# Second layer: products of turned rows with seven weights as three fp32r products of exact halves

## The reference

```python
x = x + attn0(layernorm(x))      # 16 heads of 8, causal softmax
x = x + moe(layernorm(x))        # 8 experts, top 2, capacity, gelu
# attn1: y = LN(h)*g+b; q,k,v = y@W + b; g = sigmoid(y@Wg + bg)  (128 -> 1024 each)
#        state = decay*state + k*v;  out = g*q*state/8;  o = out@Wo + bo
#        x2 = h + o;  return x2 + gelu(LN(x2)@W1 + b1)@W2 + b2   (128 -> 512 -> 128)
x = x + attn1(layernorm(x))
# ffn1:  h = silu(x@w1.T*s1) * (x@w2.T*s2); h = gelu(h@h1.T*..); h = gelu(h@h2.T*..); h@w3.T*s3
x = x + ffn1(layernorm(x))
```

## Time and profile before

| | |
|---|---|
| median of 3 runs | 770.17 us (768.14 to 771.0) |
| the profiled execution | 770.86 us, its span 768.8 us |
| mean granted TensorE clock | 0.933 of full speed |
| busy: TensorE / VectorE / ScalarE / GpSimd | 633.4 / 398.5 / 260.2 / 141.6 us |
| the chain that ended last | TensorE 61%, VectorE 19%, issue 8%, GpSimd 6%, ScalarE 5% |

### The profile page before, as it was taken

The page is one execution under the profiler, slowest core; times in us unless marked ns, Lnnn a source line. Parts: engine busy times, 40 slices in busy tenths (PEclk is TensorE's granted clock), DMA queues, the critical chain, the costliest instruction groups (busy, mean ns, idle before and its releaser), DMA issues.

```text
span 768.8 us, 8745 instructions
## 1 busy us (share of the span) xinstructions
PE 633.4 (82%) x2992; PEld 376.8 (49%) x2992; DVE 398.5 (52%) x1008; ACT 260.2 (34%) x342; POOL 141.6 (18%) x169
## 2 busy tenths in 40 slices
PE   2579999799798408989609779999999999999997
PEld 0545556456455306777504255364545455464544
DVE  6677778777786321111046955944385616831100
ACT  2325454445345102333103214422534135412311
POOL 3002212332432540000054073011000300010000
PEclk9989999899999657999958988999999999999999
DMA  5223242342410201443110011000000000000000
GB/s 153 90 72 133 103 152 75 93 162 63 134 60 1 82 31 48 124 123 106 35 27 28 0 28 28 0 1 1 14 0 0 0 14 1 0 1 1 14 0 14
DMA packets 40900, 38.69 MB, mean 50 GB/s; under 512 B 3104, under 2 KB 31776, under 8 KB 40864
## 3 DMA queue, kind: packets, MB, share of 16 engines
q1 hardware_dynamic: 38816, 34.04, 14.3%
q0 software_dynamic: 2048, 4.20, 1.8%
HBM read 23.54 MB, written 14.68 MB: 50 GB/s over the span
## 4 chain that ended last, share of the span: by engine, by line
PE 61%; DVE 19%; issue 8%; POOL 6%; ACT 5%; DMA 1%; DVEq 0%; ACTq 0%; POOLq 0%
PE ps L1417 16%; PE ps L1403 7%; PE ps L1410 6%; PE ps L1376 5%; PE ps L1367 5%; PE ps L1217 5%; PE ps L1188 4%; DVE pm L817 3%; PE ps L1205 3%; DVE V L1043 3%; POOL xs_dram L451 2%; PE ps L1449 2%; DVE V L1047 2%; DVE OG L1040 2%; PE ps L1450 2%
## 5 line engine op out<-in xcount | busy, mean ns | idle before, releaser
L817 DVE TENSOR_REDUCE pm<-ps 128x4 f32<-128x512 f32 x160 | 104.7, 687 | 28.0 <-PE ps L1191 17.8
L1417 PE MATMUL ps<-PT,fh 128*128 128x512 f32 x256 | 111.6, 594 | 2.5 <-ACT PT L666 1.6
L575 ACT ACTIVATE PT<-ps 128x768 f32<-128x768 f32 (+1 forms) x96 | 84.6, 882 | 84.0 <-PE ps L1205 83.3
L1188 PE MATMUL ps<-KP,QS 128*128 128x512 f32 x160 | 69.4, 462 | 12.1 <-DVE pm L817 10.4
L1417 PEld LDWEIGHTS ps<-PT,fh 128*128 128x128 f32 x256 | 48.0, 190 | 62.0 <-issue 57.4
L666 ACT ACTIVATE PT<-ps,cols 128x512 f32<-128x512 f32 x48 | 32.8, 687 | 120.8 <-PE ps L1417 120.7
L460 POOL TENSOR_SCALAR_AFFINE_SELECT PT<-PT 128x512 f32<-128x512 f32 x64 | 39.9, 635 | 171.1 <-ACT PT L575 171.1
L444 POOL TENSOR_TENSOR rstd<-veps,mhalf 128x4 f32<-128x4 f32 x20 | 21.7, 1084 | 256.9 <-DVE veps L745 256.8
L1205 PE MATMUL ps<-QM,KP 128*128 128x512 f32 (+3 forms) x256 | 62.7, 347 | 1.1 <-DVE QM L831 1.1
L1217 PE MATMUL ps<-PT,V 128*32 128x128 f32 (+3 forms) x512 | 46.3, 456 | 10.8 <-POOL PT L460 10.8
L1188 PEld LDWEIGHTS ps<-KP,QS 128*128 128x128 f32 x160 | 30.4, 199 | 42.6 <-DVE pm L817 40.9
(11 more groups left out here) (162 smaller groups left out, 925.8 us busy)
## 6 DMA issues: line engine op xcount, KB each, us to landing
qk_dram<-HL SPq DMA_DIRECT2D x8, 512.0 KB, 3.4
PT<-in_eW SPq DMA_DIRECT2D x16, 256.0 KB, 3.4
QS<-qk_dram SPq DMA_DIRECT2D x64, 48.0 KB
KP<-qk_dram SPq DMA_DIRECT2D x64, 48.0 KB
xs_dram<-zero SPq DMA_DIRECT2D x4, 640.0 KB, 5.4
PT<-xs_dram SPq DMA_DIRECT2D x8, 320.0 KB, 3.8
ys_dram<-zero SPq DMA_DIRECT2D x8, 320.0 KB, 2.9
qk_dram<-HL SPq DMA_DIRECT2D x8, 256.0 KB, 3.7
```

Source lines behind the costliest of these rows:

```text
L575: act.activation(PT[:, 2 * i:2 * i + 2, a:z], ps[:, 2 * (n % 2) + 2:2 * (n % 2) + 4, 0:z - a], ACT.Exp, scale=float(DK) ** -0.5).then_inc( ...
L817: v.tensor_reduce(pm[:, t, k, :], bank[n % 2].rearrange("p (i n) -> p i n", n=P), AXX, ALU.max).then_inc(pair_free[n % 2], 1)
L1188: mm = pe.matmul(to, QS[:, G % 2, t * P:(t + 1) * P], KP[:, G % 3, k, :, :].rearrange("p i n -> p (i n)"), start=True, stop=t != k)
L1417: mm = pe.matmul(bank[6 + n % 2], w, x, start=(i == 0), stop=(i == len(products) - 1))
```

## The change

Each of the seven weights is held as a high half, rounded to fp32r, and a low half, the rest. Each turned tile is split in the same way. A product w*x becomes three fp32r products added up in the same bank: high*high, low*high, high*low.

- The transfers of the seven weights go to tiles that are free then (`HT`, `xnT`). After the last routing ScalarE writes the high halves with seven Copies (into `KP`), VectorE the low halves with seven subtractions (into `lw`, `lw1`, `fw1`, `fw2`). ScalarE waits for `w_low` before the experts.
- `turned` writes `turned_full`, waits for its own instruction, and makes the high half with a Copy (`hi_done`). GpSimd makes the low half (`low_half`, `lo_done`). ScalarE waits for `lo_done` of the tile before. The halves lie in `QS` and `QM`.
- Where a turned tile is new (`project1` with n, `hidden1`, w1/w2), TensorE issues the products with its high half first, for two f (or four banks), waits for `lo_done`, and then issues those with the low half. In other `project1` calls the three products of a bank follow one another.

```diff
+            def low_half(n, halves_of):
+                g.wait_ge(hi_done, n)
+                g.tensor_tensor(halves_of[1], turned_full, halves_of[0].bitcast(F32), ALU.subtract).then_inc(lo_done, 1)
...
             add_bo(0)
+            low_half(1, aT)
             gather(1)
             gather_end(1)
             rsqrt(varC, rsC, 3)
             rsqrt(varC, rsC, 4)
             gather(2)
+            low_half(2, aT)
             rsqrt(varC, rsC, 5)
             add_b2(0)
+            low_half(3, aT2)
 
             add_bo(1)
             gather_end(2)
...
                 rsqrt(varC, rsC, VAR(b))
+                low_half(TURN(b), aT2)
                 if attn:
                     rsqrt(varC, rsC, VAR(b) + 1)
                     add_b2(b + 1)
+                    low_half(TURN(b) + 1, aT2)
                 if prep:
                     rsqrt(varC, rsC, VAR(b) + 2)
                     rsqrt(varC, rsC, VAR(b) + 3)
                     add_bo(b + 2)
+                    low_half(TURN(b) + 2, aT)
...
             gate_exp(NB - 1)
+            act.wait_ge(w1_in, 16 * 23)
+            for high, whole in zip(highs, loaded):
+                act.activation(high, whole, ACT.Copy).then_inc(w_high, 1)
+            act.wait_ge(w_low, len(lows))
...
-            def turned(n, dst, **kw):
+            def turned(n, halves_of, **kw):
                 act.wait_ge(t_full, n)
-                act.activation(dst, bank[4], ACT.Identity, **kw).then_inc(t_done, 1)
+                if not isinstance(n, int) or n > 1:
+                    act.wait_ge(lo_done, n - 1)
+                act.activation(turned_full, bank[4], ACT.Identity, **kw).then_inc(t_done, 1)
+                act.wait_ge(t_done, n)
+                act.activation(halves_of[0], turned_full, ACT.Copy).then_inc(hi_done, 1)
...
+            for k, (high, whole) in enumerate(zip(highs, loaded)):
+                v.wait_ge(w_high, k + 1)
+                v.tensor_tensor(lows[k][0][:, :], whole, high.bitcast(F32), ALU.subtract).then_inc(w_low, 1)
...
+            def high_products(to, high, low, halves_of):
+
+                pe.matmul(to, high, halves_of[0], start=True, stop=False)
+                pe.matmul(to, low, halves_of[0], start=False, stop=False)
+
+            def low_product(to, high, halves_of):
+                return pe.matmul(to, high, halves_of[1], start=False, stop=True)
...
+            def project1(c, f, n=None):
+                cs = slice(f * P, (f + 1) * P)
+                if n is not None:
+                    pe.wait_ge(hi_done, n)
+                    for m, (name, done) in enumerate(PROJECTIONS):
+                        pe.wait_ge(done, c * LF + f)
+                        high_products(bank[m], lwh[name][:, cs], lw[name][:, cs], aT)
+                    pe.wait_ge(lo_done, n)
+                    for m, (name, done) in enumerate(PROJECTIONS):
+                        low_product(bank[m], lwh[name][:, cs], aT).then_inc(qkvg, 1)
+                    return
+                for m, (name, done) in enumerate(PROJECTIONS):
                     pe.wait_ge(done, c * LF + f)
-                    pe.matmul(bank[m], lw[n][:, f * P:(f + 1) * P], aT[:, :], start=True, stop=True).then_inc(qkvg, 1)
-
+                    high_products(bank[m], lwh[name][:, cs], lw[name][:, cs], aT)
+                    low_product(bank[m], lwh[name][:, cs], aT).then_inc(qkvg, 1)
+
+            def hidden1(at, n):
+
+                pe.wait_ge(hi_done, n)
+                for fs in ((0, 1), (2, 3)):
+                    for f in fs:
+                        cs = slice(f * P, (f + 1) * P)
+                        pe.wait_ge(hid_done, at + f)
+                        high_products(bank[6 + f % 2], lw1h[:, cs], lw1[:, cs], aT2)
+                    pe.wait_ge(lo_done, n)
+                    for f in fs:
+                        low_product(bank[6 + f % 2], lw1h[:, f * P:(f + 1) * P], aT2).then_inc(hid_full, 1)
...
+                pe.wait_ge(hi_done, TURN(b))
+                for fs in ((0, 1), (2, 3)):
+                    for f in fs:
+                        cs = slice(f * P, (f + 1) * P)
+                        if f >= 2:
+                            pe.wait_ge(sl_done, b * FF + f - 1)
+                            pe.wait_ge(a_done, b * FF + f - 1)
+                        elif attn:
+                            pe.wait_ge((v_done, k_done)[f], (b + 2) * LF)
+                            pe.wait_ge((g_done, q_done)[f], (b + 2) * LF)
+                        high_products(bank[f % 2], fw1h[:, cs], fw1[:, cs], aT2)
+                        high_products(bank[2 + f % 2], fw2h[:, cs], fw2[:, cs], aT2)
+                    pe.wait_ge(lo_done, TURN(b))
+                    for f in fs:
+                        cs = slice(f * P, (f + 1) * P)
+                        low_product(bank[f % 2], fw1h[:, cs], aT2).then_inc(a_full, 1)
+                        low_product(bank[2 + f % 2], fw2h[:, cs], aT2).then_inc(a_full, 1)
```

More of the change, by code:

```diff
@@ L221, in build @@
         rx = VR[:, 3 * TB:4 * TB, :]
-        aT = zero[:, 0:SEQ]
+        turned_full = zero[:, 0:SEQ]
+        lows = [(lw[n], LF * P) for n in ("Wv", "Wk", "Wg", "Wq")] + [(w, FF * P) for w in (lw1, fw1, fw2)]
+        KPflat = KP[:, :, :, :, :].rearrange("p s k i n -> p (s k i n)")
+        ends = [sum(n for _, n in lows[:k + 1]) for k in range(len(lows))]
+        highs = [KPflat[:, z - n:z] for z, (_, n) in zip(ends, lows)]
+        loaded = [HTflat[:, 0:LF * P], HTflat[:, LF * P:2 * LF * P], HTflat[:, 2 * LF * P:3 * LF * P],
+                  HTflat[:, 3 * LF * P:4 * LF * P], xnT[:, 0:FF * P], HTflat[:, 4 * LF * P:4 * LF * P + FF * P],
+                  HTflat[:, 4 * LF * P + FF * P:4 * LF * P + 2 * FF * P]]
+        lwh = dict(zip(("Wv", "Wk", "Wg", "Wq"), highs))
+        lw1h, fw1h, fw2h = highs[4:]
+        aT = (QS[:, 0, :], QS[:, 1, :])
         vs = xnT[:, 0:0 + 2 * SEQ].rearrange("p (a n) -> p a n", a=2)
@@ L1423, in layer1 @@
                 if not last:
-                    pe.wait_ge(t_done, TURN(b) - 1)
-                    for f in range(FF):
-                        hidden(f, [(lw1[:, f * P:(f + 1) * P], aT2)])
+                    hidden1(b * 12, TURN(b) - 1)
                 if attn:
@@ L1460, in layer1 @@
                 if early:
-                    pe.wait_ge(t_done, TURN(b) + 1)
-                    for f in range(FF):
-                        hidden(8 + f, [(lw1[:, f * P:(f + 1) * P], aT2)])
+                    hidden1(b * 12 + 8, TURN(b) + 1)
                     pe.wait_ge(hid_done, b * 12 + 13)
@@ L1486, in _ @@
             turn(2, xp)
-            pe.wait_ge(t_done, 2)
-            project1(1, 0)
+            project1(1, 0, 2)
             turn(3, xn)
```

45 lines of the change are left out of this document (17 added, 28 removed).

## The result

The changed kernel takes 782.98 us (median of 4, 781.43 to 783.94), the kernel before 769.5 us (median of 4, 768.14 to 771.0). The ratio is 1.0173, 95% interval 1.0144 to 1.0202: slower by 13.5 us, inside the range, 4.8 us above the forecast of 778.2. The profiled execution has a span of 782.1 us against 768.8.

A forecast was written before the change was run, and what follows sets the result against it. The prediction took VectorE as the bound, or level with TensorE, in layer 2's attention stage; added terms summed to 8.0 us, so 778.2 us against the median of 770.17, range 768 to 786.

The forecast's parts named there:

- rival that TensorE was the bound: Layer 2: TensorE sets the pace, so most of 28 us comes off, 744 us in all; chance 0.08.
- rival that the clock falls in the attention stage: Attention stage: less busy TensorE drops to 1.2 GHz and becomes the bound, 800 us in all; chance 0.08.
- cancelling rival: Split and attention: no shared-port holds; wave order costs half; +3.3 us, 773.5 us in all; chance 0.20.
- the split: Weight split before the experts: VectorE's subtractions hold GpSimd's scatters, +1.5 us.
- the holds: Three attention stages: GpSimd's low-half subtraction holds VectorE's work, 0.5 us each, +1.5 us.
- the unrolled `hidden1`: `hidden1` in the unrolled block: Copy and low half delay its products while TensorE idles, +1.6 us.
- the last w1/w2: w1/w2 products of the last block: nothing hides ScalarE and VectorE behind them, +0.7 us.
- The w1/w2 products in the loop: w1/w2 stage, three times: low products of f=0 come behind the high ones of f=1, +0.55 us each.
- the prologue: Prologue of layer 2, up to the addition of 475.05: +1.0 us, bounds 0 to 3.
- TensorE regains this on the cheap products: Start of blocks 1 and 2: cheaper products win back the later gelu, 0 us, bounds -1 to +0.5.
- The two steps and the gain ahead of the turn at 463.71: Prologue: VectorE's second tile +1.3, normalisation +1.3, apply beside one GpSimd addition fewer -1.2 us.
- The stretch behind it: Prologue, from that turn to the addition: Copy +0.8, cheaper following tile and `to_rows` -4 x 0.16, giving 0.2 us.

The follow-up runs named there:

- e4: Changed kernel without the rows' low half: two products per weight (high*high, low*high), no GpSimd subtraction, no waves; 759.34 us, ratio 0.9854.
- e5: As e4, but only the product of the high halves (high*high) is made; 760.62 us, ratio 0.9880.
- e3: Changed kernel with VectorE's seven weight subtractions moved behind the scatters, weights loaded to other tiles in another order; 781.25 us, ratio 1.0165.
- e9: e4 plus a third product that reads the rows' high half again, so no low half is computed or waited for; 764.19 us, ratio 0.9941.
- e1: Changed kernel with ten products that nobody reads between the two pairs of `hidden1` products in rounds 0, 1 and 2; 786.03 us, ratio 1.0185.
- e7: Changed kernel with GpSimd's `low_half(2)` in the prologue moved behind the reciprocal root `rsqrt(5)`; 782.15 us, ratio 1.0175.
- e8: Changed kernel with ScalarE writing the high half straight from the PSUM bank first, then the full tile; 779.99 us, ratio 1.0144.
- e2: Changed kernel without waves (prologue and early `hidden1` keep them): TensorE waits for the low half, then finishes bank after bank; 774.35 us, ratio 1.0035.
- e11: e10 plus ten products that nobody reads in TensorE's gap, as in e1, round 0 in the prologue included; 755.29 us, ratio 0.9811.
- e10: e4 with one activation at each turn, from bank to high half, and the weight subtractions behind the scatters as in e3; 752.03 us, ratio 0.9776.
- e6: Changed kernel with the edits of e2, e3, e7 and e8 together; 769.24 us over 12 executions, ratio 1.0000.

## Why the prediction was right, and where not

The direction was right, and for its reason: the stage in which TensorE looks full is VectorE's, and the cheap products win nothing there. The rival that TensorE was the bound (744) falls with the step of VectorE's tiles, which is the same before, in e4 and in e5, and but for one hold a block in the changed kernel, and with e5's time: it takes two thirds of the changed products' TensorE work away and lands 1.3 us above e4. The rival that the clock falls in the attention stage (800) falls with the window at 1.00 and 18.02 of 23.01 us busy. With eight products a tile instead of twelve it did fall there (e4, 0.50 from 566.9 to 570.3), and VectorE kept its step. The cancelling rival (773.5) falls with the scatters of 1.97 and 1.43 us and the hold of 1.13.

By terms: the split (forecast 1.5, measured 1.3, shown by e3), the holds (1.5 and 1.4), the unrolled `hidden1` (1.6 and 1.5; 0.2 in e9, which has no waves and no low half to wait for) and the last w1/w2 (0.7 and 0.7) stand. The w1/w2 products in the loop were forecast at 0.55 each and took 0.74.

The rows that the prediction quoted for the hold (2.06 against 1.12 us) are of an instruction with one input tile, not of "two-input work"; for that the first evidence is the rows at 580. The Trainium skill (SBUF — State Buffer, Who interferes with whom) says that a VectorE instruction with two SBUF inputs contends with a GpSimd instruction that reads SBUF, and calls the shared port pair an exclusive lock; that the other engine is blocked for the whole instruction it says of another mode of VectorE. Taken over to this case it would give 0.58 us at 580.75, what was left of GpSimd's 1.29. The row shows 0.44 (1.13 less 0.69). All four such rows of the changed kernel are 0.14 or 0.15 us below what was left; the longest is in the prologue:

```profile
466.38 1.28 POOL L520 TENSOR_TENSOR QM<-zero,QM 128x512 fp32r<-128x512 f32 x1 [3.58 <-ACT QM L677]
466.39 1.81 DVE L1084 SCALAR_TENSOR_TENSOR PT<-V 128x512 f32<-128x512 f32 x1
```

There 1.27 us were left and the hold is 1.12. The rule is right in kind and a little high.

The step that failed is "TensorE regains this on the cheap products", with its 0 and bounds of -1 to +0.5, at the start of a block. ScalarE's chain came as it was walked. The price put on the products behind it took the full clock for granted: they met 1.2 GHz, and 1.80 and 1.9 us were lost, outside the bound. e1 shows 1.45 and 1.55 of these as the clock, and 0.36, inside the bound, as what the walk costs without it. As the same gap was followed by full clock in round 1 of e3, e7 and e8, a profile of the changed kernel could as well have shown only one of the two falls: how close the total came to the forecast is in part luck. I had the clock as a rival for the attention stage only, and did not ask what each newly opened gap does to the stretch behind it.

In the prologue 1.0 became 2.4, inside its bounds of 0 to 3. The prediction's own steps (1.3 + 1.3 - 1.2 + 0.8 - 0.64) add up to 1.6 and not 1.0. The two steps and the gain ahead of the turn at 463.71 were to give 1.4 and gave 1.6. The stretch behind it was to give 0.2 and gave 0.8; a longer cold stretch is the likely cause, not shown.

And the forecast priced the wave order as given. It is the largest single cost of the change (e2). Its 0.55 for the w1/w2 stage was worked out against the kernel before. Set against the order without waves, which gains 1.0 where the waves lose 0.74, it is 1.7 at each w1/w2.

## What to carry to other kernels

When a product gets cheaper in a stage where another engine sets the pace, the gain is a gap, not time. Look at each gap that opens: what does TensorE run right behind it, and is that on the path? Price that stretch at both clock levels. A filler for the gap is not free: where the clock is already low and the next products are ready, it stands in front of them (1.8 us in e11's prologue).

Splitting a sum into waves to hide a late operand delays the first finished bank and holds the others. Where the next engine takes banks one by one and the late operand is there in time, wait for it and finish bank after bank. (The waves of the prologue and of the unrolled `hidden1`, where the operand is late, stayed in every run with three full products, so their worth is not shown.)

A half made by a third engine (bank to ScalarE to GpSimd to TensorE) costs at every place where nothing else runs: here 1.5 us at the unrolled `hidden1`. Ask whether one activation from the bank can make all that the product needs.

## What the runs showed of the hardware

- After a gap of 2.7 us in TensorE's work the granted clock fell to 0.50 for some 3 us in rounds 1 and 2 of the changed kernel, in round 2 alone of e3, e7 and e8, in both rounds of e4 (gaps of 2.5 us, the fall 1.2 to 1.5 us behind them) and in neither start of e10 (gaps of 2.5 and 2.4 us). Behind gaps of 1.3 us at the same place it stayed up in both rounds of e2, e6 and e9. After a gap of 1.8 us it fell in e1, e7 and e8, not in e3 or the changed kernel. The gap alone does not tell whether it falls.
- A scatter issue of GpSimd is held by VectorE's two-input work (1.97, 1.43 for 0.96 us), and VectorE by GpSimd's (1.12 to 1.81 for 0.69 us). With VectorE's work moved away all scatters took 0.96 again (e3).
- The start of ScalarE behind a turn, 0.64 us in some kernels, was 2.2 to 5.4 us in others at the same place, with no releaser in the view. This is open.
- With the same instructions ahead of it, one scatter started between 272.9 and 277.0 us in the profiles of eight kernels. This is open too.
